# An fp32 attention layer on one core: half of the next input's low parts on VectorE, its loads and a weight load moved to other units

## The reference, cut to what matters

```python
qkv = (xr @ w_qkv + b_qkv).reshape(B, S, N_HEADS, 3 * d_k)      # 8 heads, d_k = 64
q, k, v = jnp.split(qkv, 3, axis=-1)
attn = jax.nn.softmax(jnp.einsum('bihd,bjhd->bijh', q, k) * scale, axis=2)
out = jnp.einsum('bijh,bjhd->bihd', attn, v).reshape(B, S, N_HEADS * d_k)
out = out @ w_proj + b_proj
return out.transpose(0, 2, 1).reshape(B, C, H, W) + x
```

## Time and profile before

| | before |
|---|---|
| median of 3 runs | 4190.05 us |
| profiled execution, its own time | 4186.1 us |
| its span, first to last instruction | 4183.9 us |
| busy: PE, DVE, ACT, POOL | 95%, 78%, 70%, 74% |
| mean granted TensorE clock | 0.982 of full speed |
| share of PE on the chain that ended last | 84% |
| instruction loads, queues q8 and q14 | 185 of 16 KB, 325 of 8 KB in the mean |

### The profile page before, as it was taken

How to read it: one execution, slowest core, us unless ns; L and a number is a source line. 1 busy time by engine, 2 the same in 40 slices (tenths; PEclk the granted TensorE clock), 3 DMA queues, 4 the chain that set the end, 5 groups by cost and what they waited for, 6 DMA issues and landing times.

```text
span 4183.9 us, 77099 instructions
## 1 busy us (share of the span) xinstructions
PE 3972.2 (95%) x18464; PEld 3383.7 (81%) x18464; DVE 3242.8 (78%) x4382; ACT 2929.9 (70%) x5527; POOL 3076.6 (74%) x2436
## 2 busy tenths in 40 slices
PE   4999999999999999999999999999999999999997
PEld 3878878888887887878878788787888878788885
DVE  3888878788787887878878788787878778787884
ACT  2777767677676776767767677676777767677774
POOL 1788777777677876777777777777777767787775
PEclk9999999999999999999999999999999999999999
DMA  6344433434343344333434344343343434334432
GB/s 179 92 109 108 132 97 92 123 101 121 97 119 95 102 133 105 107 103 98 129 100 112 101 102 118 102 135 96 95 120 104 121 95 110 105 102 124 117 82 70
DMA packets 263566, 455.18 MB, mean 109 GB/s; under 512 B 107920, under 2 KB 118160, under 8 KB 258960
## 3 DMA queue, kind: packets, MB, share of 16 engines
q1 hardware_dynamic: 263056, 449.48, 40.1%
HBM read 206.58 MB, written 41.42 MB: 59 GB/s over the span
## 4 chain that ended last, share of the span: by engine, by line
PE 84%; issue 6%; POOL 4%; DVE 2%; ACT 1%; DMA 1%; SPq 1%; POOLq 0%; DVEq 0%; ACTq 0%
PE ps_g L396 23%; PE s L418 10%; PE st L471 10%; PE ps_o L528 10%; PE ps_o L530 10%; PE st L469 10%; PE ps_g L412 9%; POOL p_hl L752 2%; PE st L515 1%; PE st L516 1%; POOL x_l L736 1%; DVE acc L653 1%; DVE nm L656 1%; ACT p_hl L592 0%; DMA rinv_d<-r 0%
## 5 line engine op out<-in xcount | busy, mean ns | idle before, releaser
L752 POOL TENSOR_TENSOR p_hl<-p,p_hl 128x512 fp32r<-128x512 f32 x2048 | 2607.6, 1296 | 1036.4 <-ACT p_hl L592 1035.6
L589 ACT ACTIVATE p<-st 128x512 f32<-128x512 f32 x2048 | 1231.1, 601 | 798.9 <-PE st L471 650.0
L656 DVE TENSOR_REDUCE nm<-s 128x1 fp32r<-128x1024 f32 x1024 | 1251.0, 1222 | 426.2 <-PE s L418 409.7
L653 DVE TENSOR_TENSOR acc<-acc,p 128x512 f32<-128x512 f32 x1792 | 1235.5, 689 | 137.3 <-issue 123.4
L592 ACT ACTIVATE p_hl<-st 128x512 fp32r<-128x512 f32 x2048 | 1236.9, 604 | 0.0
L469 PE MATMUL st<-q,k 128*128 128x512 f32 x2048 | 799.8, 391 | 17.5 <-issue 17.3
L528 PE MATMUL ps_o<-p_hl,v_hl 128*128 128x512 f32 x2048 | 805.6, 393 | 5.2 <-POOL p_hl L752 4.5
L471 PE MATMUL st<-q,k 128*128 128x512 f32 x2048 | 803.5, 392 | 0.0
L530 PE MATMUL ps_o<-p_hl,v_hl 128*128 128x512 f32 x2048 | 802.5, 392 | 0.0
L396 PE MATMUL ps_g<-x_h,wq 128*128 128x512 f32 x2016 | 715.8, 395 | 29.9 <-POOL x_l L736 29.8
L418 PE MATMUL s<-k,q 128*128 128x512 f32 x2048 | 655.4, 401 | 83.0 <-DVE nm L656 80.6
(11 more groups left out here) (79 smaller groups left out, 3714.9 us busy)
## 6 DMA issues: line engine op xcount, KB each, us to landing
wq<-wq_d SPq DMA_DIRECT2D x128, 512.0 KB, 5.1
k<-qk_h SPq DMA_DIRECT2D x256, 256.0 KB, 4.3
wv<-wv_d SPq DMA_DIRECT2D x32, 1024.0 KB, 5.1
q<-qk_h SPq DMA_DIRECT2D x128, 256.0 KB, 3.8
q<-qk_l SPq DMA_DIRECT2D x128, 256.0 KB, 4.9
k<-qk_l SPq DMA_DIRECT2D x128, 256.0 KB, 5.2
q<-q SPq DMA_DIRECT2D x256, 128.0 KB, 4.0
rinv<-rinv_d SPq DMA_DIRECT2D x256, 128.0 KB, 2.8
```

What stands on the lines that cost most here:

```text
L589: nc.scalar.activation(p[:, to, :], st[slot % RING][:], ACT.Exp)
L653: nc.vector.tensor_tensor(acc[:], acc[:], probs, ALU.add).then_inc(acc_done, 1)
L656: nc.vector.tensor_reduce(nm[:, it:it + 1], s1[:], AXX, ALU.max, negate=True).then_inc(max_done, 1)
L752: nc.gpsimd.tensor_tensor(p_l[:, to, :], p[:, to, :], p_h[:, to, :].bitcast(f32), ALU.subtract).then_inc(pl_done, 1)
```

## The change

Chunks with `c % 4 < 2` stay with GpSimd; the low parts of chunks 2, 3, 6 and 7 go to VectorE, in the same units, ahead of VectorE's part of a group. The semaphore `x_low` becomes two, one for each engine, and the three waits on it are rewritten. The loads of chunks 0, 1 and 2 are issued in units 41, 42 and 43 instead of all in unit 40. `load_wq` goes from `u == 0` to `u == 3`, behind `load_max`.

```diff
-    X_LOAD = {40: (0, 1, 2)} | {42 + c: (c,) for c in range(RING, CHUNKS)}
+    X_LOAD = {41: (0,), 42: (1,), 43: (2,)} | {42 + c: (c,) for c in range(RING, CHUNKS)}
+    X_POOL = [c for c in range(CHUNKS) if c % KT < 2]
...
-                    if u == 0 and B.on(h + 3, HEADS):
-                        sp.wait_ge(qk_done, at(2 * HEADS, 2 * (h + 1) + 2))
-                        load_wq(h + 3)
...
                     if u == 3 and B.now:
                         sp.wait_ge(max_stored[1], at(16 * HEADS, 16 * (h + 1)))
                         load_max(1)
+                    if u == 3 and B.on(h + 3, HEADS):
+                        sp.wait_ge(qk_done, at(2 * HEADS, 2 * (h + 1) + 2))
+                        load_wq(h + 3)
...
-                        sp.wait_ge(x_low, at(CHUNKS, CHUNKS + max(0, c - RING + 1)))
+                        if c >= RING:
+                            i = (c - RING) % KT // 2
+                            sp.wait_ge(x_low[i], at(KT, KT + (c - RING) // KT * 2 + (c - RING) % 2 + 1))
+                        elif c == 0:
+                            sp.wait_ge(x_low[1], at(KT, KT))
...
-                                pe.wait_ge(x_low, at(CHUNKS, CHUNKS + KT * (n + 1)))
+                                for j in range(2):
+                                    pe.wait_ge(x_low[j], at(KT, KT + 2 * (n + 1)))
...
+                    if U in X_SPLIT and B.ahead and X_SPLIT[U] not in X_POOL:
+                        c = X_SPLIT[U]
+                        k, n = c % KT, c // KT
+                        dve.wait_ge(x_high, at(CHUNKS, CHUNKS + c + 1))
+                        nc.vector.tensor_tensor(xs[1][:, k, cols(n)], ring[c % RING][:], xs[0][:, k, cols(n)].bitcast(f32),
+                                                ALU.subtract).then_inc(x_low[1], 1)
...
-                    if U in X_SPLIT and B.ahead:
+                    if U in X_SPLIT and B.ahead and X_SPLIT[U] in X_POOL:
```

More of the change, by code:

```diff
@@ L187, in attention_kernel @@
         x_high = sem("x_high")
-        x_low = sem("x_low")
+        x_low = [sem(f"x_low{i}") for i in range(2)]
         qk_done = sem("qk_done")
@@ L420, in first_scores @@
                 return mm
-            pe.wait_ge(x_low, CHUNKS)
+            for i in range(2):
+                pe.wait_ge(x_low[i], KT)
             for i in range(QK0):
@@ L736, in split_x @@
                 nc.gpsimd.tensor_tensor(xs[1][:, k, cols(n)], src, xs[0][:, k, cols(n)].bitcast(f32),
-                                        ALU.subtract).then_inc(x_low, 1)
+                                        ALU.subtract).then_inc(x_low[k // 2], 1)
             for i, c in enumerate(X_FIRST):
```

## The result

| | before | after |
|---|---|---|
| median | 4188.37 us (4 runs) | 4086.11 us (4 runs, 4082.26 to 4088.27) |
| ratio to before, 95% interval | | 0.9756 [0.9739, 0.9773] |
| span of the profiled execution | 4183.9 us | 4083.5 us |
| busy: PE, DVE, ACT, POOL | 95%, 78%, 70%, 74% | 97%, 81%, 72%, 74% |
| PE busy | 3972.2 us | 3944.9 us |

The change makes the kernel faster by 2.4%, 102 us; 118 were forecast (4072 us). In the changed kernel the lines of interest are L424 (was L418), L402 (L396), L664 (L656), L661 (L653), L642 (L634), L740 (L726), L722 (L714) and L766 (GpSimd's low parts of the probabilities, L752); L727 is new, VectorE's low part of a chunk.

What follows compares the result with a forecast made beforehand. TensorE, 95% busy, was taken as the bound, so only its waits counted. −67 − 19 − 22 − 10 = −118 from the profiled 4186.1 us gave 4068, as a median 4072 us; own range 4050 to 4090, with rivals 4048 to 4128.

Steps and rivals of the forecast that it cites:

- VectorE's code: At the 13 loop jumps: four more instructions ahead of VectorE's loop remove L418's wait for its maximum, −67 us.
- The second gap: VectorE's 5.79 us standstill after the loop's first instruction at a jump, read as waiting for a second block of code.
- Rival A: At the jumps, VectorE's loop head does not come free; moved weights still help: median 4123 us, chance 0.14.
- the 5 us that I left for the jumps: L418's remaining wait at the jumps, 0.4 us at each of 13, since the first gap differs between jumps.
- The clock: TensorE's slow clock: −19 us behind the jumps (of 25.6), −10 behind the `x_l` waits (of 11.3).
- Weights and chunk loads: Moving the weights' load to `u == 3` and chunks 0 to 2 to later units: 0 us.
- Rival C: In the unit after `u == 3`, `s64` comes late behind the weights: slower, median 4259 us at 7.5 us landing, chance 0.04.
- Low parts: TensorE's 15 waits in unit 52 fall from 2.03 to 0.5 us with VectorE's low parts: −22 us.
- the three other subtractions of an input: VectorE's low parts in units 46, 47, 50 fit its idle time, 0.85 us a unit; uncovered, up to 34 us.
- Rival B: In unit 51 VectorE's subtraction waits for GpSimd's normalization, so the `x_l` wait only changes owner: median 4104 us, chance 0.13.
- The 0.10 us that I read at the start: GpSimd subtraction beside a VectorE group at the start: 1.36 against 1.26 us, taken as at most partial blocking.

Runs made afterwards that it cites:

- e1: The kernel before with one more VectorE instruction ahead of its loop (first memset in two halves), nothing else: 4104.55 us, ratio 0.9801.
- e3: The changed kernel with 124 more VectorE instructions ahead of the loop, its head 128 further than in the kernel before: 4138.45 us, ratio 0.9887.
- e4: The changed kernel with the weights' load (`load_wq`) back in `u == 0`: 4085.28 us, ratio 0.976.
- e2: The kernel before with only the weights' load (`load_wq`) moved to `u == 3`: 4160.67 us, ratio 0.9931.
- e7: The changed kernel, VectorE's low-part subtraction replaced by an operation with one PSUM and one SBUF input (results wrong, time only): 4070.93 us, ratio 0.9719.
- e5: The kernel before with the edits of e1 and e2, all low parts on GpSimd: 4106.32 us, ratio 0.9808.
- e6: e5 with the next input's chunks loaded and split one unit earlier: 4065.48 us, ratio 0.9704.
- e8: e6 with sixteen more VectorE instructions ahead of the loop than the kernel before, in place of one: 4061.39 us, ratio 0.9703.

## Why the prediction was right or wrong

*VectorE's code, −67: right, −66.* The second gap went away because the head left the last place of a block. e1 (alone it does it), e3 (128 further it is undone), the 13 loads on q14 that go and come back with it, and the changed kernel's chain (0.05 us in place of 5.79) show it. Rival A, that the head does not come free, is refuted by the same. Of the 5 us that I left for the jumps, 5.3 came, though as waits for `v_hl` and not at L418.

*The clock, −19 and −10: right in the sum, in part by luck.* PE is busy 27.3 us less; 29 were forecast. But I had 25.6 + 11.3 = 37 us as the whole loss and kept some 8 of it, and nothing stayed: the trace before has 20 stretches at half clock between 95 and 4120 us (the 13 jumps and the 7 waits), the changed kernel's has none between 95 and 4030. The whole was 27, some 10 us less than I worked out, and the two errors nearly cancel.

*Weights and chunk loads, 0: right.* e4 shows it for the weights: they matter only while a second block is waited for, and then 26 us (e2; 30 in rival A's sum). That the chunk loads cost nothing is not shown apart; no wait of the changed kernel names them. Rival C, a late `s64`, is refuted by one wait of 3.2 us in the run, the one that was there before.

*Low parts, −22: the term that failed; −6.6.* For the profiled execution 4068 us were forecast and 4085.3 measured; 15 of these 17 us are this one term. I had the subtraction at 0.75 us, after `qk_l`, and left 0.5 us in unit 52; and I let "the three other subtractions of an input" lie "in VectorE's idle time". Both prices are those of an operation alone, and the row that I took, `qk_l`, has PSUM as one of its inputs. Beside GpSimd the subtraction took up to 1.84 us, and unit 47 has no idle time for 1.72: `stage` came late there, and I had that at nothing. It cost 11.2 us: 0.63 us in unit 48 of 14 inputs, and in nine of them 0.28 more in unit 50; both are gone in e7. `qk_l` cost 12.0 where 7.5 were left. e7 shows it: with 0.69 us everywhere `stage` waits no more than before and the term is −29.8 + 9.9 = −19.9, near the forecast's −22; the time is 4070.9, near its 4072. Of the excess over 7.5 in `qk_l`, 2.1 us belong to it and 2.4 to my estimate.

Rival B had the mechanism and the wrong place. I looked for it in unit 51, where VectorE in fact comes ahead of the normalization and holds it up, and takes itself only 0.25 us more than alone, beside the low part of the probabilities; it decided in unit 47, where GpSimd is first and VectorE waits out nearly a whole instruction. The Trainium skill's page "SBUF — State Buffer", section "Who interferes with whom", says that a VectorE instruction with two SBUF inputs contends with a GpSimd instruction that reads SBUF, and calls the ports that they share an exclusive lock. The trace agrees: 1.72 against 0.68 us, and 1.73 against 1.31 on GpSimd's side; and e7, with one SBUF input, shows none of it (0.691 to 0.693). The 0.10 us that I read at the start against the full rule came from an overlap of 0.23 us at the end of VectorE's group, too short to show it; it is not the only one, as the three other subtractions from `p` in the start also begin at the end of a group of VectorE, and take 1.36 to 1.40 us. B's 4104 was too high since the waits did get shorter, in unit 52 from 2.03 to 0.82 us.

## What to carry to other kernels

Where an engine stands in "issue" at each jump of a hardware loop and one instruction runs between two gaps, count its instructions up to the loop's head and move the head by a few; here one instruction was worth 82 us of 4186. An operation that goes to another engine is priced with its neighbours: a VectorE subtraction of two SBUF tiles beside GpSimd is not 0.7 us but up to 1.8, and what stands behind it decides. Before moving work to another engine, see whether it can begin a unit earlier: that gave twice and more what the move gave (e5 to e6 41 us, e5 to the changed kernel 20 at most).

## What the hardware showed unexpectedly

A load of code brings 128 instructions of VectorE (8 KB on q14), and the head's place within these 128 set 2% of the time of a kernel of 77099 instructions. The end of the loop counts too: where the loop's last few instructions lie just behind a block's edge, a load of code goes out 0.1 us ahead of the jump, and the first gap is 4.6 us instead of 4.1 (e6, e8); in e6 the loop is 645 instructions long and its head is the first of a block, so the last 5 stand behind an edge. In time that was worth nothing that could be measured. VectorE and GpSimd hold each other up in both directions, and which one pays is set by who starts first, 0.1 us apart here: 0.68 us on VectorE and 1.75 on GpSimd in unit 46, 1.72 and 1.28 in unit 47.
